# One schedule table, three edits: the last full FFN brought forward, two VectorE operations a little later, one ScalarE copy ahead of an exponential

## The reference

```python
x = x + attn_a(layernorm(x))   # 16 heads of 64, softmax, exact gelu, projection, its own residual
x = x + ffn(layernorm(x))      # ternary weights, 256 -> 1024, relu, 1024 -> 256, bias
x = x + attn_b(layernorm(x))   # 16 heads of 16, biases, rotary embedding, softmax
x = x + ffn(layernorm(x))      # the same FFN again
```

## The kernel before

| phase | engine | what |
|---|---|---|
| 38 | VectorE | `parts_low` of the second query half (`LOWS[1]`, L1154, reads `q_rot` and `roped_q`) |
| 39 | VectorE | `statistics` of ffn1, first half (`NORM["ffn1"][0]`, L1122) |
| 40 | GpSimd | `add_bias` for ffn0 (`BIAS`, L563, `x_ahead`) |
| 40, 41 | VectorE | low parts of the transposed ffn0 input (`empty_low`, L1219, `xl`) |
| 41 | VectorE | `invert_sums` (L1199, L1201) |
| 44, 45 | VectorE | `statistics` second half; `aggregate` (L1122, L1128 to L1131) |
| 46 | GpSimd | `inverse_deviation` of ffn1 (L554, `rstd`) |
| 46 | VectorE | `parts_low` of the last key half; ScalarE's `hidden_high` (L919, `h_hi`) of ffn0's first tile waits for it |
| 47 | GpSimd | `hidden_low` (L569, `h_lo`) of that first tile |
| 49, 51 | VectorE | `normalise` of ffn1, two tiles each (L1136, `xn`) |
| 12 | ScalarE | `exps`, then `hidden_high` of ffn1's last (eighth) tile |
| 13 | VectorE | `first_hidden_low` of that tile (L1175, `h_lo`); the first `down` product waits for it |

## Time and profile before

### The profile page before, as it was taken

One profiled execution on the slowest core, in us unless ns is written; L12 is line 12 of the kernel. 1 busy time (PEld: TensorE's weight loads), 2 busy tenths in 40 slices (PEclk: granted clock), 3 DMA queues, 4 the chain that ended last, 5 costly groups with the idle time before them and its releaser, 6 DMA issues.

```text
span 3779.0 us, 64440 instructions
## 1 busy us (share of the span) xinstructions
PE 3626.6 (96%) x23810; PEld 2433.1 (64%) x23810; DVE 2584.8 (68%) x4296; ACT 2385.9 (63%) x4629; POOL 1888.6 (50%) x1337
## 2 busy tenths in 40 slices
PE   8999999999999999999999978999999999999987
PEld 6777777777777777777777664555555555555534
DVE  6766666666667666666767656777777777777763
ACT  5665656556566566655656546777777777777754
POOL 4555555556555555555654633444444444444412
PEclk9999999999999999999999998999999999999989
DMA  2000000000000000000000012222222222222220
GB/s 79 7 12 1 12 12 12 1 12 12 1 12 12 1 12 12 9 5 12 12 1 15 25 43 47 53 62 62 63 62 61 61 63 58 62 59 64 53 48 18
DMA packets 102329, 116.27 MB, mean 31 GB/s; under 512 B 23557, under 2 KB 75269, under 8 KB 102021
## 3 DMA queue, kind: packets, MB, share of 16 engines
q1 hardware_dynamic: 102020, 112.17, 12.0%
HBM read 34.48 MB, written 27.26 MB: 16 GB/s over the span
## 4 chain that ended last, share of the span: by engine, by line
PE 76%; DVE 11%; ACT 7%; issue 5%; POOL 1%; DMA 0%; DVEq 0%; ACTq 0%; SPq 0%
PE ps_o L675 12%; PE ps_s L644 10%; PE ps_t L657 8%; PE ps_t L226 8%; PE ps_m L657 4%; PE ps_o L751 4%; PE ps_t L233 4%; DVE max_b L1160 4%; PE ps_t L786 4%; PE ps_m L226 3%; PE ps_t L710 3%; PE ps_s L724 3%; ACT et L867 2%; PE ps_m L233 2%; PE ps_s L738 2%
## 5 line engine op out<-in xcount | busy, mean ns | idle before, releaser
L534 POOL TENSOR_TENSOR e_a<-e_a,recip 128x1024 f32<-128x1024 f32 x512 | 969.4, 1894 | 948.7 <-DVE recip L1027 948.5
L825 ACT ACTIVATE e_a<-ps_s,neg_max 128x512 f32<-128x512 f32 x1024 | 695.1, 685 | 544.8 <-DVE neg_max L1020 544.4
L1160 DVE TENSOR_REDUCE max_b<-ps_s 128x2 f32<-128x1024 f32 x512 | 625.0, 1221 | 270.6 <-PE ps_s L724 268.8
L867 ACT ACTIVATE et<-ps_s 128x1024 f32<-128x1024 f32 x512 | 527.4, 1030 | 319.9 <-PE ps_s L738 319.0
L1020 DVE TENSOR_REDUCE neg_max<-ps_s 128x2 f32<-128x1024 f32 x512 | 623.0, 1217 | 67.7 <-PE ps_s L644 67.7
L675 PE MATMUL ps_o<-et_a,v_a 128*64 128x256 f32 x4096 | 499.8, 386 | 9.1 <-DVE heads_a L1063 4.8
L644 PE MATMUL ps_s<-raw_a 64*128 64x512 f32 x3072 | 425.9, 409 | 5.5 <-ACT e_a L825 5.3
L675 PEld LDWEIGHTS ps_o<-et_a,v_a 128*64 128x64 f32 x4096 | 279.2, 137 | 192.1 <-issue 78.3
L657 PE MATMUL ps_t<-ident,e_a 128*128 128x128 f32 x2660 | 394.0, 280 | 2.1 <-DVE xl L1219 2.0
L1034 DVE COPY et_a<-ps_t 128x512 f32<-128x512 f32 x366 | 251.1, 688 | 206.3 <-PE ps_t L657 202.1
L657 PEld LDWEIGHTS ps_t<-ident,e_a 128*128 128x128 f32 x2660 | 290.1, 141 | 133.2 <-issue 129.3
(11 more groups left out here) (194 smaller groups left out, 7231.0 us busy)
## 6 DMA issues: line engine op xcount, KB each, us to landing
q_stack<-roped_q SPq DMA_DIRECT2D x256, 96.0 KB
k_stack<-roped_k SPq DMA_DIRECT2D x256, 96.0 KB
x_a<-X SPq DMA_DIRECT2D x16, 512.0 KB, 3.4
X<-x_a SPq DMA_DIRECT2D x16, 512.0 KB, 2.9
x_ahead<-X SPq DMA_DIRECT2D x16, 512.0 KB, 3.8
X<-x_ahead SPq DMA_DIRECT2D x16, 512.0 KB, 2.9
x_before<-X SPq DMA_DIRECT2D x16, 512.0 KB, 3.9
OUT<-x_before SPq DMA_DIRECT2D x16, 512.0 KB, 5.2
```

The lines of the kernel that those rows point to most:

```text
L534: nc.gpsimd.tensor_tensor(e_a[:, u % 5, :, :], e_a[:, u % 5, :, :], factor, ALU.mult).then_inc(e_normed, 1)
L825: ins = nc.scalar.activation(e_a[:, u % 5, h, :], ps_s[:, 2 * (u % 2) + h, :], ACT.Exp, bias=neg_max[:, u % 5, h:h + 1], accum_out=sums[:, ...
L867: nc.scalar.activation(et[:, v % 5, :, :], ps_s[:, 2:4, :], ACT.Exp)\
L1160: nc.vector.reduce_max(max_b[:, u // 4 % 2, :, u % 4], ps_s[:, score_bank(u):score_bank(u) + 2, :], AX.X, negate=True).then_inc(max_done, 1)
```

## The change

- Sequence 14's second FFN gets a table of its own (`WO_EARLY` and so on): `wo` at steps 991 to 995 (before: 994 to 1002), statistics 995 and 997, normalising 1000 and 1001, transposes 1003 and 1004 (before 1014, 1015), `up` 1006 to 1015 (before 1024 to 1034), `down` 1017 to 1023 (before 1036 to 1044), the save at step 1026 (before 1048).
- In every pass the first ffn1 statistics move from phase 39 to 43, the second from 44 to 45, the aggregation from 45 to 46 on VectorE, and with it the inverse deviation from 46 to 47 on GpSimd.
- `parts_low` of the second query half moves from phase 38 to 40.
- TensorE's transposes wait for `xn` tile by tile in the first of each two instead of for all four.
- ScalarE makes the high part of an FFN's last tile ahead of the step's exponentials. That changes an order only where the step is even: ffn1's last tile, at phase 12, in sequences 0 to 13.

```diff
-        NORM = {..., "ffn1": (103, 108, 109, 113, 115)}
+        NORM = {..., "ffn1": (107, 109, 110, 113, 115)}
+        WO_EARLY, XT_EARLY, FFN_EARLY = (95.5, 96.5, 98.5, 99.5), (107.1, 108.1), (99, 101, 102, 104, 105)
+        UP_EARLY, DOWN_EARLY = (110.1, 111, 112, 113.5, 115, 116.5, 118, 119), (121.5, 123.5, 125.5, 127)
+        BIAS_EARLY, SAVE_EARLY = 107, 130
...
-        ROTATE, HIGHS, LOWS = (...), (-31, -29, -23, -21), (-28, -26, -20, -18)
+        ROTATE, HIGHS, LOWS = (...), (-31, -29, -23, -21), (-28, -24, -20, -18)
...
                     elif kind == "transpose":
-                        pe.wait_ge(xn_ready, TB * (nth_norm[part, s] + 1))
                         for t in range(TB):
+                            if i == 0:
+                                pe.wait_ge(xn_ready, TB * nth_norm[part, s] + t + 1)
...
+                        for kind, part, i, s, fill in steps_of.get(step - 2, []):
+                            if kind == "up" and i == FT - 1:
+                                hidden_high(part, i, s, fill)
                         if step % 2 == 0 and 0 <= step // 2 - L < UNITS_ALL:
                             exps(step // 2 - L)
                         for kind, part, i, s, fill in steps_of.get(step - 2, []):
-                            if kind == "up":
+                            if kind == "up" and i < FT - 1:
                                 hidden_high(part, i, s, fill)
```

More of the change, by code:

```diff
@@ L308, in hybrid_block_kernel @@
         UP1, DOWN1 = (128, 129, 130.5, 132, 133, 134.5, 136.5, 138.5), (140.5, 142.5, 146.5, 148.5)
-        NORM = {"ffn0": (-101, -100, -98, -93, -91), "attn": (-67, -64, -63, -51, -49), "ffn1": (103, 108, 109, 113, 115)}
+        NORM = {"ffn0": (-101, -100, -98, -93, -91), "attn": (-67, -64, -63, -51, -49), "ffn1": (107, 109, 110, 113, 115)}
+        WO_EARLY, XT_EARLY, FFN_EARLY = (95.5, 96.5, 98.5, 99.5), (107.1, 108.1), (99, 101, 102, 104, 105)
+        UP_EARLY, DOWN_EARLY = (110.1, 111, 112, 113.5, 115, 116.5, 118, 119), (121.5, 123.5, 125.5, 127)
+        BIAS_EARLY, SAVE_EARLY = 107, 130
         UP_RAMP, DOWN_RAMP, XTB_RAMP = tuple(range(-66, -58)), (-57, -55.5, -54, -52.5), (-45.9, -44.9)
@@ L312, in hybrid_block_kernel @@
         BIAS = {"ffn0": -88, "attn": -45, "ffn1": 124}
-        ROTATE, HIGHS, LOWS = (-39, -37, -35, -34, -32, -30), (-31, -29, -23, -21), (-28, -26, -20, -18)
+        ROTATE, HIGHS, LOWS = (-39, -37, -35, -34, -32, -30), (-31, -29, -23, -21), (-28, -24, -20, -18)
         STACK = (-17, -15, -11, -9, 5, 7, 21, 23)
@@ L326, in hybrid_block_kernel @@
             plan += [(VB[t], "v", "attn", t, s) for t in range(TB)]
[L327 to L330, removed]
+            early = s == BATCH - 2
+            plan += [((WO_EARLY if early else WO1)[t], "wo", "ffn1", t, s) for t in range(TB)]
+            plan += [((XT_EARLY if early else XT1)[k], "transpose", "ffn1", k, s) for k in range(KT)]
+            plan += [((UP_EARLY if early else UP1)[f], "up", "ffn1", f, s) for f in range(FT)]
+            plan += [((DOWN_EARLY if early else DOWN1)[t], "down", "ffn1", t, s) for t in range(TB)]
         plan = sorted((SLOT * s + at_step, kind, part, i, s) for at_step, kind, part, i, s in plan)
@@ L354, in norm_at @@
         def norm_at(part, s):
-            return ATTN_RAMP if (part, s) == ("attn", 1) else NORM[part]
+            if (part, s) == ("attn", 1):
+                return ATTN_RAMP
+            return FFN_EARLY if (part, s) == ("ffn1", BATCH - 2) else NORM[part]
         norms = sorted((SLOT * s + norm_at(part, s)[0], part, s) for s in range(BATCH) for part in NORM)
@@ L524, in _ @@
                                 load_before(s)
-                            if r == 152:
+                            if r == (SAVE_EARLY if s == BATCH - 2 else 152):
                                 save_before(s)
@@ L620, in _ @@
                             for part in NORM:
-                                if r == BIAS[part]:
+                                if r == (BIAS_EARLY if (part, s) == ("ffn1", BATCH - 2) else BIAS[part]):
                                     add_bias(part, s)
```

## The result

| | us |
|---|---|
| median of 4 runs after the change (3822.36 to 3829.72) | 3823.41 |
| the kernel before, 4 runs beside it | 3783.49 |
| ratio, with its 95% interval | 1.0109 (1.0092 to 1.0127) |
| forecast, and its range | 3808 (3781 to 3837) |

A forecast was written before the change was run, and what follows sets the result against it. With TensorE busy 96% of the span, its waits, mostly for VectorE's maxima, and the end bound the kernel. Passes 22.9, clock 6.5 and end -3.5 gave +25.9 us on 3781.2: 3807.1, median 3808.2, range 3781 to 3837.

The forecast's parts named there:

- The held low part: VectorE's moved low part is held until GpSimd's bias add ends, making unit 406's scores late: +1.36 us a pass.
- 0.43 given back: At unit 413, TensorE's wait for ScalarE's backlog goes when TensorE is late: -0.43 us a pass.
- Aggregation ahead of the last key part: In phases 42 to 46 VectorE's last low part ends later, delaying ScalarE's first `h_hi` of ffn0: +0.54 us a pass.
- The `xn` behind `h_lo`: Ahead of unit 409's maximum, VectorE's `xn` wait for GpSimd's inverse deviation, queued behind `h_lo`: +0.55 us a pass.
- the second pair: VectorE's second two `xn` beside GpSimd's `h_lo`: taken at 0, with 1.3 us kept for the range.
- The high part first: At unit 390 TensorE's wait for the low part shrinks: -0.26 us (to -0.51) for 14 sequences.
- The clock: The 2.35 us wait lowers TensorE's clock more often: 0 to 19.5 us, a third taken, +6.5 us.
- The end: Sequence 14's earlier FFN, earlier load and tile-wise waits shorten the run's end: sum -5.0, taken as -3.5 us.
- GpSimd's bias and VectorE's norm lie in slots with room: At the end, the moved FFN's bias (2.4 us) and norm find room; attention there ends 3.3 us earlier.
- (a): Rival: low part and `xn` are not held in the passes, so the change gains: -13.8 us, 3768; chance 0.11.
- (b): Rival: low part slips through, but the inverse deviation stands behind `h_lo`: about 3783 us; chance 0.12.
- (c): Rival: forecast's mechanisms without clock, 3801; with it in all passes and second `xn` pair held, 3838; 0.77 together with forecast.

The follow-up runs named there:

- e2: The changed kernel with ffn1's statistics and aggregation back at phases 39, 44 and 45: 3807.04 us, ratio 1.0053.
- e1: The changed kernel with the second query half's low part back at phase 38: 3783.14 us, ratio 0.9988.
- e5: The changed kernel with GpSimd's inverse deviation ahead of the low part of ffn0's first tile in its step: 3820.08 us, ratio 1.0090.
- e9: The kernel before with one edit, the last hidden tile's high part ahead of the exponentials: 3779.12 us, ratio 0.9978.
- e10: The changed kernel with TensorE computing the fourth `wo` product of a sequence twice, inside the wait at unit 406: 3814.56 us, ratio 1.0084.
- e3: The changed kernel with both VectorE moves (low part; statistics and aggregation) taken back: 3780.59 us, ratio 0.9985.
- e7: The kernel before with only sequence 14's early second FFN and the waits tile by tile: 3787.72 us, ratio 1.0007.
- e13: e3 with unit 511's scores computed three times more in the even slots 512 to 522: 3778.37 us, ratio 0.9976.
- e6: The kernel before with one edit, the second query half's low part at phase 40 instead of 38: 3815.83 us, ratio 1.0080.
- e11: The kernel before with high part first, tile-wise waits, low part at phase 40, bias add at 39, statistics at 43 and 44: 3779.97 us, ratio 0.9987.
- e4: The changed kernel with ffn0's bias add one phase earlier on GpSimd (39 instead of 40): 3781.28 us, ratio 0.9993.

## Why the prediction was right, and where its sizes were off

The list of TensorE's waits in a pass leaves out one of 0.54 us, for exponentials, 51 us behind unit 403's maximum; it is as long after the change.

**The held low part: right.** Its place, its length, the moment of unit 405's maximum and the wait of 2.35 us came out to the hundredth or two. For the pass it is +1.17 in e2, where the forecast has 1.36, or 0.93 with its 0.43 given back.

**Aggregation ahead of the last key part: there, at about the price,** 0.67 where it has 0.54, but only on top of the held low part; without that, e1 has it and all that follows for 0.11. ScalarE waits 1.55 us for it (1.42 before).

**The `xn` behind `h_lo`: mechanism right, price in the wrong place.** For the first pair the forecast took 0.55: `h_lo` starts 0.06 or 0.07 us ahead of the `xn` in every pass and holds it, VectorE's 1.80 us wait and TensorE's 0.49 us are there, and yet a pass without the second collision pays only 0.14 (e5). The step that failed is the one that let only 0.43 us be given back: the maximum of unit 410 is 3.43 us late and that of unit 413 1.98, so 1.45 us come back. For the second pair the forecast saw the tie, took 0 and kept 1.3 us for the range. The runs have both outcomes: nine passes at no cost, four at 1.1 us each, 4.4 us in all, that the sum took at nothing.

**The high part first: right,** -0.36 where it has -0.26, and nothing for the later exponentials. In sum a pass without a fall of the clock was to grow by 1.76 us and grew by 1.62.

**The clock: mis-sized, and the main miss.** "I take a third" of 19.5 us; it fell in 12 of 13 passes at 1.2 us each (95.23 against 94.01). That is 14.7 us, or 13.2 more than before with its one fall, instead of 6.5. The price of a fall was near (1.1 to 1.3 in e2, 1.0 to 1.2 in most passes after, against 1.5 from one pass); the number was not. The one fall before with a wait of 1.09 us already said that this place is at the edge, and a wait of twice that was past it nearly everywhere. In the slots behind unit 467 the clock was lower as well (0.76 against 0.82 in the windows up to unit 491), for 2.7 us that the forecast doesn't have. This stretch varies with the execution, from 65.5 to 70.5 us over all traces, the longer the lower its clock; e9, without any move, has 70.1 at 0.81. That the change causes it is not shown.

**A pass left out.** The bias add stands in sequence 0's pass too, the low part is held there (2.45 us), TensorE waits 2.8 us behind it, the longest wait of the list, and by unit 51 the kernel is 3.3 us late. From unit 19 to 51 it takes 91.2 us in the kernel after, e2, e5 and e10, which hold it, and 87.7 or 87.8 in the kernel before, e3, e7 and e13, which don't. Part of this is clock: e1 and e9 hold nothing and have 91.3 and 90.3 with more of the pass at 1.2 GHz. The forecast counted 13 passes because it looked for the statistics, which sequence 0's pass doesn't have.

**The end: mechanisms half there, the number by luck.** Behind the last `weighted` it is 1.8 us shorter, where the forecast has 1.7 (0.9 and 0.8). The residual add waits for TensorE now instead of the load and starts 1.0 us earlier:

```profile
3787.58 0.69 DVE L1196 TENSOR_TENSOR x_before<-x_before,ps_m 128x512 f32<-128x512 f32 x1 [4.01 <-PE ps_m L773]
...
3793.93 1.35 PE L778 MATMUL ps_t<-ident,xn 128*128 128x128 f32 x4 [4.49 <-DVE xn L1146]
```

But TensorE was at 1.2 GHz for 6.8 us here (3.4 before), so the second residual add waits 1.28 us for it, and the first `xn` comes 12.63 us behind the last `weighted`, against 12.54 before: the 0.9 us didn't arrive. The first transpose starts 0.9 us earlier, while `xn` are made, and the first `down` 0.3 us. The other 1.5 us come in the `down` products, of which 3.4 us ran at 1.2 GHz before and none after. e6, without any of the edits of the end and without a fall in `down`, has this shorter time too (40.4 us behind the last `weighted`, against 42.3 before and 40.5 after).

From unit 491 to the last `weighted` it is 0.6 us, not 3.3. The step that failed is "GpSimd's bias and VectorE's norm lie in slots with room". The earlier `wo` of sequence 14 meets the load of its own `x_before`, issued only after sequence 13's was stored. Timeline after, SyncE, VectorE and TensorE:

```profile
3713.64 0.38 SPq L447 DMA_DIRECT2D x_before<-X  x1
...
3717.39 0.69 DVE L1196 TENSOR_TENSOR x_before<-x_before,ps_t 128x512 f32<-128x512 f32 x1 [2.31 <-DMA x_before<-X]
...
3721.74 0.50 PE L730 MATMUL ps_s<-k_stack,q_stack 48*128 48x512 f32 x2 [1.73 <-DVE max_b L1170]
```

The add waits 2.31 us in VectorE's order ahead of the maxima, and TensorE then 0.47 and 1.73 us for those. The change has moved the buffer's wait from sequence 15 to sequence 14. Even the 0.6 us may be the clock: over the traces this stretch takes 77.4 to 87.6 us with the early end (ten kernels) and 77.2 to 83.4 without (four).

**Sum.** Forecast +25.9 on the profiled time, measured +42.3 in the span. The 13 passes have 9.3 of the difference (38.7 against 22.9 and 6.5): 6.7 from the falls, 4.4 from the four held second pairs, less 1.8 because a pass without either grew by 1.62 and not 1.76. The pass left out has 3.3, the slots behind them 2.7, the end 1.2 (2.3 instead of the 3.5 taken).

**The rivals.** (a) had 3768 for a change in which nothing is held; no kernel came near it, since the moves win nothing even then (e11). (b), the queue alone without the held low part, had 3783; e4 is just that and measured 3781. Its sum has a slip: 0.7 us less 0.43 and 0.26 is 0.01 us a pass and not 0.3, which gives 3779. (c) had 3838, 1 us above the forecast's range, with the clock down in all passes and every second pair held by two; the kernel came to 12 and 4 of 13. What told (b) from the forecast was the 0.46 us between the start of the bias add and the low part's issue.

## What to carry to other kernels

When a VectorE operation with two inputs in SBUF is moved, look at what GpSimd does at the new place, not only at VectorE's own load: here 0.68 us became 2.46, and one step of the table on GpSimd instead made it vanish. A wait that appears on TensorE in one piece can have a second price, the clock; count the places where it recurs. Where two operations that can't run side by side become ready together, reckon with both outcomes, and look at every pass: one pass of the trace shows only one of them. A buffer that is freed earlier at one end of its cycle may be wanted earlier at the other.

## What the runs showed of the hardware that I had not expected

TensorE's granted clock falls at waits of 1.5 to 2.35 us in a stretch that is otherwise busy. Among 13 equal passes it fell in none with waits up to 0.7 us, in none or one with up to 1.1 us, in 4 with 1.50 us, in 6 and 8 with 1.96 us, in 10 and 12 with 2.35 us, each time to 1.2 GHz for 3.4 us or more, at 0.7 to 1.6 us of a pass's time (2.2 us in the one pass where it lasted 6.8 us). Filling the 2.35 us wait with matmuls that nobody needs cut the falls from 12 to 4.

A held VectorE operation gets its turn at the end of GpSimd's current operation even if GpSimd has the next one ready: two `xn` (0.36 us alone) beside a run of `h_lo` end one behind each `h_lo` (2.77 us for the two), each 0.15 us behind it, and not behind the run of four. The hold goes both ways, and hundredths of a microsecond decide it: the two start within 0.03 us of each other, and in nine passes of 13 it is the `h_lo` that is longer (1.48 us instead of 1.29), in four the `xn` (1.46 instead of 0.36).
